# Two sets of q and k halves a layer, a loop over pairs of steps, and a new order of tasks in a two-layer attention kernel

## The chip, the cores and the metric

The kernel runs on one core of a Trainium2 chip. The metric is the device time of one execution in microseconds (us). The engines are PE (TensorE), ACT (ScalarE), DVE (VectorE), POOL (GpSimd) and SP (SyncE, which here only issues transfers). Each has its own in-order stream of instructions; they wait for one another through semaphores.

## The reference

Sixteen batches of x (256 rows of 512) go through four residual blocks; the context has 384 columns.

```python
x = x + _L0_xattn_ref(_layernorm(x, axis=-1), ctx_768, ctx_768, ...)   # q and k l2-normalised over 512, 16 heads of 32,
                                                                       # then out @ Wo + bo + Qp and a layer norm
x = x + _L0_ffn_ref(_layernorm(x, axis=-1), L0_ffn_weight)             # Hadamard, 4-bit levels per row, ternary weight
x = x + _L1_xattn_ref(_layernorm(x, axis=-1), ctx_768, ...)            # scores clipped, softmax, values, Wo
x = x + _L1_ffn_ref(_layernorm(x, axis=-1), W1, b1, W2, b2)            # ternary 512 -> 2048, gelu, ternary 2048 -> 512
```

## The kernel before

The first three blocks are one pipeline over batches, the last one (the FFN with 2048 columns) a second phase behind it, which the change doesn't touch. The rows of a batch are two tiles of 128 (`NT = 2`). Nearly all products are made of float16 halves: a value is split in an upper half (ACT rounds it) and a lower half (DVE subtracts), and three products are summed.

The work of a batch in the pipeline is four lists of tasks, the streams: 0 is layer 0's front (`front_0`: load of x and context, statistics, turns, projections of q, k and v, norms, turned and split q and k), 1 is layer 0's heads and back (`heads_of(0) + back(0)`: scores, exponentials, values, output projection, norm, then the Hadamard, level and ternary product of the small FFN, and the store of x1), 2 is layer 1's front (with `maxima`, products of scores only for the row maxima, and `reduce` on DVE), 3 is layer 1's heads and back (`clip` on DVE, `head`, output, store of x2). They are called 0f, 0b, 1f and 1b. In a step i of the pipeline 0f works on batch i, 0b on i-1, 1f on i-2 and 1b on i-3. Steps 0 to 3 are written out, steps 4 to 15 are a hardware loop (`steps`, `eng.Fori`), steps 16 to 18 are written out again with fewer streams active.

How the four lists are merged is a string of digits, `ORDER`: each digit says from which list the next task is taken. All engines walk the same merged list, and each issues its part of every task. The eight banks of PSUM are given out along this list too (`banks_of`): a task that fills a bank waits on PE until the bank's last reader is done (`open_bank`, semaphore `bankN_read`).

Task `head l n` is itself a small pipeline: ACT makes the exponential of head n (128x512 in float32, in a ring of `NF` buffers `pf`) and then the upper half (`ph`) of head n-1; POOL makes the lower half of head n-1 (L776); PE makes the product with the values for head n-4 (L1483 to L1485), and for layer 1 first a pair of products that subtracts the row maximum (L1465); DVE divides after every fourth head (`attn_out`, L1216, L1219). Scores come in quads of four heads, which use 32 rows of PE each (L1450).

The halves of turned q and k lie in one buffer a layer (`qk_raw`), so a batch's `split_qk` waits until the heads of the batch before are through (`p_hi`). Two buffers `spare` and a buffer `signs_raw` are used for weights: at the start for staging (`stage_w`), in steps 16 to 18 for the weights of the large FFN (`wb`, `wb_signs`), whose mean magnitude DVE sums in step 16 (`mean_part`, L1015, one at each second head of layer 0) and whose signs it makes in step 18. The levels of the small FFN, and then x1, are made in `tq`, which is the same memory as layer 0's attention output (`out0`).

Transfers: SP walks the same list. `load l` brings x and context (l = 0) or the context's turned halves and x1 (l = 1) of the batch, `fetch l` the residual of the back (and for l = 0 a copy of q inside SBUF); x1 is stored by POOL's queue (`store_x1`), x2 by SP's (L696).

## Time and profile before

| | |
|---|---|
| runs of the kernel | median 2068.04 us, 2066.56 to 2070.59 (3 runs) |
| the profiled execution | 2063.8 us, of which the span of the profile is 2062.1 |
| PE busy | 1787.1 us, 87% |
| DVE busy | 1333.4 us, 65% |
| ACT busy | 997.2 us, 48% |
| POOL busy | 897.2 us, 44% |
| PE, mean granted clock | 0.928 |

The shares are means over stages. PE's products are pipelined and their ends are modelled, so a product shows some 0.38 us where the next one starts after 0.22: the distance of starts tells what it costs. "issue" in place of a releaser means that the engine waited for nothing that the profile shows. Line numbers are those of the kernel before; a register wait shows as a row of kind ISA or REGISTER_ALU in the order.

### The profile page before, as it was taken

How to read it: one execution, taken by the hardware profiler on the slowest of the kernel's cores; microseconds unless marked ns; L12 is line 12 of the kernel's file. 1: busy time of each engine (PE TensorE's matmuls, PEld its weight loads, DVE VectorE, ACT ScalarE, POOL GpSimd, SP SyncE). 2: the span in 40 equal slices, each digit the busy share in tenths (PEclk: the TensorE clock that was granted, in tenths of full speed). 3: DMA queues.
4: the chain of work that ended last, by engine and by line, in shares of the span. 5: the costliest groups of instructions: out<-in, count | busy, mean ns of one | idle time of the engine just before them, and what ended most of it. 6: DMA issues, size and time to landing. Idle time of an engine off the chain costs nothing.

```text
span 2062.1 us, 49947 instructions
## 1 busy us (share of the span) xinstructions
PE 1787.1 (87%) x18714; PEld 1078.6 (52%) x18714; DVE 1333.4 (65%) x2518; ACT 997.2 (48%) x1858; POOL 897.2 (44%) x909
## 2 busy tenths in 40 slices
PE   4569898899988989889898899958746999999998
PEld 2335566565665756556565565635533444444443
DVE  4545787777877868778687786867586434444442
ACT  3534747566474665746657476544434222222221
POOL 1434638366382653737447374443423212222221
PEclk9679899998998999999999998969978999999999
DMA  4210202202021020210202112060232011111100
GB/s 161 98 49 27 86 12 87 71 27 97 2 96 71 27 97 1 97 70 28 96 2 97 55 43 96 2 233 1 91 128 72 1 42 41 41 41 41 41 21 21
DMA packets 48609, 124.12 MB, mean 60 GB/s; under 512 B 5644, under 2 KB 9868, under 8 KB 47384
## 3 DMA queue, kind: packets, MB, share of 16 engines
q1 hardware_dynamic: 46104, 112.64, 15.5%
q0 software_dynamic: 2304, 8.39, 1.0%
q8 instruction: 177, 2.90, 0.6%
q14 instruction: 24, 0.20, 0.0%
HBM read 81.17 MB, written 31.46 MB: 55 GB/s over the span
## 4 chain that ended last, share of the span: by engine, by line
PE 54%; DVE 19%; issue 11%; POOL 6%; DMA 4%; DVEq 2%; ACT 2%; SPq 1%; POOLq 0%; ACTq 0%
PE psum L1512 8%; PE psum L1502 8%; PE psum L1322 5%; PE psum L1302 5%; PE psum L1450 4%; PE psum L1303 4%; PE psum L1306 4%; POOL arena L776 3%; PE psum L1405 3%; DVE arena L1120 2%; DVE arena L1036 2%; DVEq L1037 2%; DMA arena<-in_ctx 2%; DVE psum L1130 2%; PE psum L1483 2%
## 5 line engine op out<-in xcount | busy, mean ns | idle before, releaser
L776 POOL TENSOR_TENSOR arena<-arena 128x512 f16<-128x512 f32 x512 | 565.2, 1127 | 242.3 <-ACT arena L924 240.0
L916 ACT ACTIVATE arena<-psum 128x512 f32<-128x512 f32 x512 | 307.3, 607 | 276.2 <-PE psum L1465 143.9
L924 ACT ACTIVATE arena<-arena 128x512 f16<-128x512 f32 x512 | 325.7, 642 | 6.8 <-PE psum L1485 6.3
L1302 PE MATMUL psum<-arena 128*128 128x512 f16 x672 | 262.0, 390 | 6.8 <-DVE arena L1047 6.3
L964 ACT ACTIVATE arena<-psum,arena 128x512 f32<-128x512 f32 x128 | 88.1, 688 | 361.3 <-PE psum L1502 361.3
L1303 PE MATMUL psum<-arena 128*128 128x512 f16 x672 | 259.4, 386 | 0.0
L1306 PE MATMUL psum<-arena 128*128 128x512 f16 x672 | 259.1, 386 | 0.0
L1512 PE MATMUL psum<-arena 128*128 128x512 f16 x1024 | 242.0, 378 | 8.9 <-DVE arena L1247 7.5
L1502 PE MATMUL psum<-arena 128*128 128x512 f16 x1024 | 243.0, 380 | 1.4 <-DVE arena L1235 1.4
L1483 PE MATMUL psum<-arena 128*128 128x33 f16 x2048 | 203.4, 182 | 41.6 <-POOL arena L776 39.6
L1450 PE MATMUL psum<-arena 32*128 32x256 f16 x4608 | 182.0, 293 | 62.6 <-issue 26.7
L1242 DVE CAST arena<-arena 128x512 f16<-128x512 f32 x128 | 72.4, 566 | 251.8 <-ACT arena L964 251.6
L806 POOL TENSOR_TENSOR arena<-arena 128x512 f16<-128x512 f32 x64 | 73.0, 1141 | 359.8 <-DVE arena L1242 359.8
L1322 PE MATMUL psum<-arena 128*128 128x128 f32 x992 | 165.6, 307 | 65.6 <-DMA arena<-in_ctx 28.2
L1483 PEld LDWEIGHTS psum<-arena 128*128 128x128 f16 x2048 | 173.5, 99 | 78.7 <-POOL arena L776 51.7
L1130 DVE TENSOR_SCALAR psum<-psum 128x512 f32<-128x512 f32 x256 | 163.3, 692 | 70.3 <-PE psum L1450 68.3
L1485 PE MATMUL psum<-arena 128*128 128x33 f16 x2048 | 199.4, 180 | 0.0
L1484 PE MATMUL psum<-arena 128*128 128x32 f16 x2048 | 199.2, 179 | 0.0
L858 ACT ACTIVATE arena<-psum 128x512 f16<-128x512 f32 (+1 forms) x192 | 110.0, 586 | 145.0 <-PE psum L1322 144.3
L1450 PEld LDWEIGHTS psum<-arena 32*128 32x128 f16 x4608 | 114.6, 99 | 123.5 <-issue 106.6
L1484 PEld LDWEIGHTS psum<-arena 128*128 128x128 f16 x2048 | 169.2, 99 | 11.1
L1322 PEld LDWEIGHTS psum<-arena 128*128 128x128 f32 x992 | 125.7, 156 | 93.3 <-issue 36.2
(117 smaller groups left out, 3255.0 us busy)
## 6 DMA issues: line engine op xcount, KB each, us to landing
arena<-x_scratch SPq DMA_DIRECT2D x48, 512.0 KB, 5.0
arena<-in_x SPq DMA_DIRECT2D x32, 512.0 KB, 5.8
arena<-in_L_ffn_W SPq DMA_DIRECT2D x16, 1024.0 KB, 5.2
arena<-arena SPq DMA_DIRECT2D x16, 512.0 KB, 5.7
x_scratch<-arena POOLq DMA_DIRECT2D x16, 512.0 KB, 3.9
x_scratch<-arena SPq DMA_DIRECT2D x16, 512.0 KB, 3.4
out<-arena SPq DMA_DIRECT2D x16, 512.0 KB, 3.2
arena<-in_ctx SPq DMA_DIRECT2D x16, 384.0 KB, 7.4
```

What stands on the lines that cost most here:

```text
L776: gp.tensor_tensor(pl[l][:, h % NP, :], pf[l][:, h % NF, :], ph[l][:, h % NP, :], ALU.subtract).then_inc(p_lo[l].sem, 1)
L916: sc.activation(pf[l][:, h % NF, :], bank(u.bank), ACT.Exp, scale=SCALE / (QS * QS) if l == 0 else SCALE).then_inc(read[u.bank], 1)
L924: sc.activation(ph[l][:, h % NP, :], pf[l][:, h % NF, :], ACT.Copy).then_inc(p_hi[l].sem, 1)
L1302: te.matmul(out, x_hi, w[:, 0, c, :], start=(c == 0), stop=False)
L1303: te.matmul(out, x_hi, w[:, 1, c, :], start=False, stop=False)
L1306: mm = te.matmul(out, x_lo, w[:, 0, c, :], start=False, stop=(c == chunks - 1))
L1322: mm = te.transpose(bank(u.bank)[:, c * P:(c + 1) * P], src[:, c * P:(c + 1) * P], ident)
L1450: mm = te.matmul(bank(u.bank)[:, k * S:(k + 1) * S], (qk_hi_t, qk_lo_t)[own][l][rows_g, j, m, k * P:(k + 1) * P], (qk_hi_t, qk_lo_t)[other ...
L1483: te.matmul(out, p_hi_t, vs[l][:, k, h, 0:OW], start=(k == 0), stop=False)
L1484: te.matmul(out[:, 0:HD], p_hi_t, vs[l][:, k, h, HD + 2:VP], start=False, stop=False)
L1502: mm = te.matmul(bank(4 + f % 2), w1T[:, c, f * P:(f + 1) * P], xTb[slot][:, part, c, :], start=(c + part == 0), stop=(c + part == DC))
L1512: mm = te.matmul(bank(k), src[:, f % NG, k * P:(k + 1) * P], w2T[:, f, :], start=(f + n == 0), stop=(f + n == FC))
```

## The change

- q and k halves: two sets a layer, chosen by the batch's parity (`halves`). `split_qk` now waits only for the heads of the batch two before. To choose the set at build time the loop's body holds two steps and runs six times.
- x1's sums and levels have a buffer of their own (`levels0`) instead of `out0`.
- The ring of exponentials `pf` has five buffers instead of four.
- To make room, `spare` and `signs_raw` are gone. Staging for weights at the start is in layer 1's halves; the large FFN's weights go through layer 0's first set and the memory of layer 0's q and k (`qk0`), which is free only when q has been copied.
- PE's waits for banks are merged where two of them concern the same bank.
- `ORDER` is a new string.

```diff
-ORDER = ("1103131313313331111010330110010000010011100110313301333133111313101331123333133311333331031230001233"
...
+ORDER = ("0211110211011300022120100100101010010111201030131000330310313031211330331332103113321212331133330132"
...
-    with eng.Fori(4, B) as i:
+    with eng.Fori(0, (B - 4) // 2) as r:
         if chain:
-            chain.offset = (i - 4) * per
-        since = {n: (i - 4) * n for n in sorted({n for x in both for n in x})}
-        emit(ALL, i, plan(ALL, base, [[since[n] for n in x] for x in both])[0])
+            chain.offset = r * (2 * per)
+        since = {n: r * (2 * n) for n in sorted({n for x in both for n in x})}
+        for odd in range(2):
+            uses = plan(ALL, plus(base, both, odd), [[since[n] for n in x] for x in both])[0]
+            emit(ALL, 2 * r + (4 + odd), odd, uses)
...
-        qk_raw = [take(2 * 2 * DC * S // 2) for _ in range(2)]
-        qk_hi_t, qk_lo_t = ([a.bitcast(F16).rearrange("p (s j m n) -> p s j m n", s=2, j=2, m=DC)[:, s] for a in qk_raw]
-                            for s in range(2))
+        qk_raw = [[take(2 * 2 * DC * S // 2) for _ in range(2)] for _ in range(2)]
+        qk_t = [[[a.bitcast(F16).rearrange("p (s j m n) -> p s j m n", s=2, j=2, m=DC)[:, s] for s in range(2)] for a in x]
+                for x in qk_raw]
         vs = [take(NT * H * VP // 2).bitcast(F16).rearrange("p (t h d) -> p t h d", t=NT, h=H) for _ in range(2)]
-        spare = [take(DC * D) for _ in range(2)]
-        signs_raw = take(DC * D)
-        NF, NP = 4, 4
+        levels0 = tiles(take(NT * D))
+        NF, NP = 5, 4
...
-        xp, tq = res0, out0
+        xp, tq = res0, levels0
...
+        def halves(l, odd, part):
+
+            return qk_t[l][(odd - ALL.index(part)) % 2]
+
...
-        stage_w = [a.rearrange("p (c n) -> p c n", c=DC) for a in spare]
+        stage_w = [a.rearrange("p (c n) -> p c n", c=DC) for a in qk_raw[1]]
...
-        wb = spare
+        wb = [qk_raw[0][0], qk0]
         wb_gt = ph_raw[0][:, 0:DC * D // 2].bitcast(F16)
-        wb_signs = [signs_raw[:, n * DC * D // 2:(n + 1) * DC * D // 2].bitcast(F16) for n in range(2)]
+        wb_signs = [qk_raw[0][1][:, n * DC * D // 2:(n + 1) * DC * D // 2].bitcast(F16) for n in range(2)]
...
                 if isinstance(i, int) and i == B:
-                    for n in range(2):
-                        load_wb(n)
+                    sp.wait_ge(p_hi[0].sem, p_hi[0].at(B - 2))
+                    load_wb(0)
...
                         fetch(l, b)
+                        if isinstance(i, int) and i == B and l == 0:
+                            sp.wait_ge(q_copied.sem, q_copied.at(B - 1))
+                            sp.wait_ge(qk_hi[0].sem, qk_hi[0].at(B - 1))
+                            load_wb(1)
...
                     elif kind == "split_qk":
-                        if not (isinstance(b, int) and b == 0):
-                            if l == 0 and at == [0, 0]:
-                                act.wait_ge(p_hi[0].sem, p_hi[0].at(b - 1))
-                            elif l == 1 and at[0] == 1:
-                                act.wait_ge(p_hi[1].sem, p_hi[1].at(b - 1, 2 * HG * (at[1] + 1)))
+                        if at == [l, 0] and not (isinstance(b, int) and b < 2):
+                            act.wait_ge(p_hi[l].sem, p_hi[l].at(b - 2))
...
                         act.wait_ge(absmax.sem, absmax.at(b, k + 1))
+                        if k == 0 and not (isinstance(b, int) and b == 0):
+                            act.wait_ge(x1_stored.sem, x1_stored.at(b - 1))
...
-                if g == 0 and l == 0 and not (isinstance(b, int) and b == 0):
-                    dve.wait_ge(x1_stored.sem, x1_stored.at(b - 1))
...
-            def open_bank(u):
-                if not (isinstance(u.free_at, int) and u.free_at == 0):
-                    pe.wait_ge(read[u.bank], u.free_at)
+            def open_banks(uses, after=()):
+
+
+                values = {u.bank: u.read_at for u in after}
+                values.update({u.bank: u.free_at for u in uses})
+                for n, value in values.items():
+                    if not (isinstance(value, int) and value == 0):
+                        pe.wait_ge(read[n], value)
+
+            def open_bank(u, *after):
+                open_banks([u], after)
...
                     elif kind == "values_ready":
-                        all_read(pe, [use["qkv", l, k, 2] for k in range(NT)])
-                        if l == 0:
-                            for k in range(NT):
-                                all_read(pe, [use["qt", 0, k, j] for j in range(2)])
+                        turned = [use["qt", 0, k, j] for k in range(NT) for j in range(2)] if l == 0 else []
+                        all_read(pe, turned + [use["qkv", l, k, 2] for k in range(NT)])
+                        pe.nop()
```

The order is seen in the engines' streams at three places. First the seam of two steps in the loop. PE, the first rows of a step; before, where L1450 is the quads of scores (layer 0, then layer 1) and L1465 the shift pair:

```order
L293 ISA
L1296 ISA [waits bank0_read]
L1296 ISA [waits bank1_read]
L1296 ISA [waits bank2_read]
L1450 MATMUL psum<-arena 128x256 [waits bank3_read]
L1450 MATMUL psum<-arena 128x256 x23
L1296 REGISTER_ALU
L1296 ISA [waits bank4_read]
L1296 REGISTER_ALU [waits bank5_read]
L1296 REGISTER_ALU [waits bank6_read]
L1450 MATMUL psum<-arena 128x256 [waits bank7_read]
L1450 MATMUL psum<-arena 128x256 x23
```

and of the change, where L1451 is the same quad and L1329 to L1333 a turned projection of layer 1's keys:

```order
L294 ISA
L1310 ISA [waits bank0_read]
L1310 ISA [waits bank1_read]
L1310 ISA [waits bank2_read]
L1451 MATMUL psum<-arena 128x256 [waits bank3_read]
L1451 MATMUL psum<-arena 128x256 x23
L1373 ISA
L1310 REGISTER_ALU [waits ctx_fetched]
L1329 MATMUL psum<-arena 128x256 [waits bank4_read]
L1331 MATMUL psum<-arena 128x256
```

Layer 1's scores have left the step's start, and two key projections of layer 1 (the second a little further on) stand there.

On DVE the same seam: the last rows of a step. Before (L1120 is `reduce`, L1146 the sum of layer 1's output):

```order
L1120 TENSOR_REDUCE arena<-psum 128x2 [waits bank7_filled]
L1119 REGISTER_ALU
L1120 TENSOR_REDUCE arena<-psum 128x2 [waits bank3_filled]
L1119 REGISTER_ALU
L1120 TENSOR_REDUCE arena<-psum 128x2 [waits bank1_filled]
L1120 TENSOR_REDUCE arena<-psum 128x2 [waits bank6_filled]
L1144 REGISTER_ALU [waits res_loaded_1]
L1146 SCALAR_TENSOR_TENSOR arena<-psum,arena 128x512 [waits bank5_filled]
L1144 REGISTER_ALU
L1146 SCALAR_TENSOR_TENSOR arena<-psum,arena 128x512 [waits bank4_filled]
```

and of the change (L1131 is `reduce`, L1105 the lower half of the values, L1194 the small FFN's output):

```order
L1105 SCALAR_TENSOR_TENSOR arena<-psum,arena 128x16x32 [waits v_hi_0]
L1193 REGISTER_ALU
L1194 SCALAR_TENSOR_TENSOR arena<-psum,arena 128x512 [waits bank2_filled]
L1130 REGISTER_ALU
L1131 TENSOR_REDUCE arena<-psum 128x2 [waits bank1_filled]
L1194 SCALAR_TENSOR_TENSOR arena<-psum,arena 128x512 [waits bank7_filled]
L1131 TENSOR_REDUCE arena<-psum 128x2 [waits bank4_filled]
L1131 TENSOR_REDUCE arena<-psum 128x2 [waits bank6_filled]
L1130 REGISTER_ALU
L1131 TENSOR_REDUCE arena<-psum 128x2 [waits bank5_filled]
```

The small FFN's output and so the store of x1 now come at the end of the step, and layer 1's output sums some 20 tasks ahead of it.

Second, SP in the loop. Before, the start of a step is `fetch 0`, then `load 0`, then `fetch 1`; `load 1` comes behind the store of the context:

```order
L639 ISA [waits x1_ready]
L639 DMA arena<-in_x 128x2x512
L640 ISA
L641 DMA arena<-arena 128x1024 [waits unit]
L652 ISA [waits qk_hi_0]
L652 DMA arena<-in_x 128x2x512
L653 ISA
L653 DMA arena<-in_ctx 128x2x384
L644 ISA
L645 ISA [waits x2_stored]
L645 DMA arena<-x_scratch 128x1024
```

and of the change, where `load 0` and `load 1` are first:

```order
L658 ISA [waits qk_hi_0]
L658 DMA arena<-in_x 128x2x512
L659 ISA
L659 DMA arena<-in_ctx 128x2x384
L662 ISA
L663 ISA [waits v_hi_1]
L664 ISA [waits ctx_stored]
L664 DMA arena<-ctx_scratch 128x768
L666 ISA [waits x1_stored]
L666 DMA arena<-x_scratch 128x1024
```

The two loads have moved ahead of the fetches, and with them the wait for the x1 store.

Third, SP at the start of step 16. Before:

```order
L613 DMA arena<-in_L_ffn_W 128x4x512 x2
L639 DMA arena<-in_x 128x2x512 [waits x1_ready]
L641 DMA arena<-arena 128x1024 [waits unit]
L645 DMA arena<-x_scratch 128x1024 [waits x2_stored]
L613 DMA arena<-in_L_ffn_W 128x4x512 [waits wb_used] x2
```

and of the change:

```order
L619 DMA arena<-in_L_ffn_W 128x4x512 [waits p_hi_0]
L664 DMA arena<-ctx_scratch 128x768 [waits ctx_stored,v_hi_1]
L666 DMA arena<-x_scratch 128x1024 [waits x1_stored]
L645 DMA arena<-in_x 128x2x512 [waits x1_ready]
L647 DMA arena<-arena 128x1024 [waits unit]
L619 DMA arena<-in_L_ffn_W 128x4x512 [waits qk_hi_0,q_copied]
L619 DMA arena<-in_L_ffn_W 128x4x512 [waits wb_used] x2
```

The second load of FFN weights has moved behind `load 1` and `fetch 0`.

## Rows read from the trace of the kernel before

**Rows 1.** Windows: the twelve loop steps, then four stretches of one step.

```profile
core 0: us, PE busy (x) PEld busy (x) DVE busy (x) ACT busy (x) POOL busy (x), PEclk, DMA share, GB/s
309.00:1351.00 1042.00, 955.57 (x12308) 627.85 (x12304) 795.01 (x1586) 643.18 (x1249) 568.81 (x600) 0.95 0.17 58
796.60:829.50 32.90, 32.82 (x278) 19.55 (x278) 27.14 (x55) 12.70 (x24) 4.21 (x5) 1.00 0.04 14
830.00:846.00 16.00, 10.73 (x186) 7.10 (x186) 7.57 (x16) 13.71 (x28) 11.50 (x12) 0.68 0.55 193
846.00:862.00 16.00, 15.84 (x313) 11.65 (x314) 10.54 (x24) 15.23 (x32) 15.34 (x15) 1.00 0.24 84
```

**Rows 2.** Timeline of SP: stores of x2, at the ends of steps 3, 15, 16, 17.

```profile
309.30 0.34 SPq L696 DMA_DIRECT2D x_scratch<-arena  x1
...
1350.79 0.36 SPq L696 DMA_DIRECT2D x_scratch<-arena  x1
1451.38 0.35 SPq L696 DMA_DIRECT2D x_scratch<-arena  x1
1512.30 0.35 SPq L696 DMA_DIRECT2D x_scratch<-arena  x1
```

**Rows 3.** The chain that ended last: start us, us on the chain, what.

```profile
798.53 0.87 PE psum L1322 x8
799.41 1.73 PE psum L1405 x8
801.57 0.11 PE psum L1312
815.05 0.77 PE psum L1450 x24
855.11 0.23 PE psum L1465 x2
```

**Rows 4.** Timeline of PE: first and last of 24 products with the values.

```profile
787.61 0.18 PE L1483 MATMUL psum<-arena 128*128 128x33 f16 x1
...
788.19 0.18 PE L1485 MATMUL psum<-arena 128*128 128x33 f16 x1
```

**Rows 5.** Timeline of POOL among the heads.

```profile
842.79 7.81 POOL L776 TENSOR_TENSOR arena<-arena 128x512 f16<-128x512 f32 x7
```

**Rows 6.** Timeline of PE: the loop's entry, and one jump back.

```profile
309.55 0.71 PE L1450 MATMUL psum<-arena 32*128 32x256 f16 x17 [0.34 <-DVE arena L1146]
...
830.84 1.48 PE L1450 MATMUL psum<-arena 32*128 32x256 f16 x45 [1.39 <-issue]
834.19 0.40 PE L1450 MATMUL psum<-arena 32*128 32x256 f16 x3 [1.87 <-issue]
```

**Rows 7.** List of waits: us in total, times, longest.

```profile
PE psum L1322 <- DMA arena<-in_ctx: 28.2, 13, 11.5
PE psum L1450 <- issue: 26.7, 22, 1.9
```

**Rows 8.** Timeline of DVE: a run of reduces.

```profile
825.81 3.24 DVE L1120 TENSOR_REDUCE arena<-psum 128x2 f32<-128x512 f32 x5
```

**Rows 9.** The page's DMA issues: KB each, median us to landing.

```profile
arena<-x_scratch SPq DMA_DIRECT2D x48, 512.0 KB, 5.0
...
arena<-in_L_ffn_W SPq DMA_DIRECT2D x16, 1024.0 KB, 5.2
arena<-arena SPq DMA_DIRECT2D x16, 512.0 KB, 5.7
x_scratch<-arena POOLq DMA_DIRECT2D x16, 512.0 KB, 3.9
...
arena<-in_ctx SPq DMA_DIRECT2D x16, 384.0 KB, 7.4
```

**Rows 10.** Timeline of DVE in step 16: first and last of eight.

```profile
1357.60 2.29 DVE L1015 TENSOR_REDUCE arena<-arena 128x1 f32<-128x2048 f32 x1 [6.86 <-DMA arena<-in_L_ffn_W]
...
1385.61 2.29 DVE L1015 TENSOR_REDUCE arena<-arena 128x1 f32<-128x2048 f32 x1 [1.63 <-DMA arena<-in_L_ffn_W]
```

**Rows 11.** DVE's normalise by line: duration ns min/median/max.

```profile
L1041 DVE TENSOR_SCALAR arena<-arena x128: 519/549/1464, 19.6 to 1976.7; 128x512 f32<-128x512 f32 x128
```

More of the change, by code:

```diff
@@ L283, in alone @@
         uses, counts = plan(active, base, None)
-        emit(active, i, uses)
+        emit(active, i, i % 2, uses)
         return plus(base, counts)
@@ L903, in step @@
                             j, m = at
-                            sc.activation(qk_hi_t[1][:, j, 2 * m:2 * m + 2, :], bank(u.bank).rearrange("p (m n) -> p m n", m=2),
+                            sc.activation(upper[:, j, 2 * m:2 * m + 2, :], bank(u.bank).rearrange("p (m n) -> p m n", m=2),
                                           ACT.Copy, scale=1.0 / WS).then_inc(qk_hi[1].sem, 1)
@@ L1103, in step @@
                         u = use["qt", l, at[0], at[1]]
+                        upper, lower = halves(l, odd, part)
                         if l == 0:
@@ L1107, in step @@
                             cols_k = slice(k * P, (k + 1) * P)
-                            v.tensor_tensor(qk_lo_t[0][:, j, :, cols_k], bank(u.bank).rearrange("p (m n) -> p m n", m=DC),
-                                            qk_hi_t[0][:, j, :, cols_k], ALU.subtract).then_inc(read[u.bank], 1)
+                            v.tensor_tensor(lower[:, j, :, cols_k], bank(u.bank).rearrange("p (m n) -> p m n", m=DC),
+                                            upper[:, j, :, cols_k], ALU.subtract).then_inc(read[u.bank], 1)
                         else:
@@ L1317, in product_turned, with turn @@
                 return mm
-            def turn(u, src, chunks):
-                open_bank(u)
+            def turn(u, src, chunks, after=()):
+                open_bank(u, *after)
                 for c in range(chunks):
@@ L1323, in turn, with step @@
                 mm.then_inc(filled[u.bank], 1)
-            def step(active, i, use):
+            def step(active, i, odd, use):
                 for part, (kind, l, *at) in task_order(active):
@@ L1372, in step @@
                     elif kind == "maxima":
-                        if k % 2 == 0:
-                            all_read(pe, [use["qt", 1, j, k // 2] for j in range(2)])
-                        products_of_quad(1, k, 0, [use["mx", 1, h] for h in quad(k)])
+                        products_of_quad(halves(1, odd, part), k, 0, [use["mx", 1, h] for h in quad(k)],
+                                         [use["qt", 1, j, k // 2] for j in range(2)] if k % 2 == 0 else [])
                     elif kind == "scores":
@@ L1378, in step @@
                             pe.wait_ge(setup_act, DC + 1)
-                        products_of_quad(l, k, 1, [use["s", l, h] for h in quad(k)])
+                        products_of_quad(halves(l, odd, part), k, 1, [use["s", l, h] for h in quad(k)])
                     elif kind == "head":
@@ L1382, in step @@
                     elif kind == "turn_out":
-                        if k == 0:
-                            all_read(pe, [use["o", l, g] for g in range(H // HG)])
-                        turn(use["ot", l, k], attn[l][:, k, :], DC)
+                        turn(use["ot", l, k], attn[l][:, k, :], DC, [use["o", l, g] for g in range(H // HG)] if k == 0 else [])
                     elif kind == "out_project":
@@ L1398, in step @@
                     elif kind == "hadamard":
-                        u = use["xf", 0, k]
-                        pe.wait_ge(read[u.bank], u.read_at)
                         u = use["had", 0, k]
-                        open_bank(u)
+                        open_bank(u, use["xf", 0, k])
                         for c in range(DC):
@@ L1415, in step @@
                     elif kind == "ffn0":
-                        u = use["nt", 0, k]
-                        pe.wait_ge(read[u.bank], u.read_at)
                         u = use["f0", 0, k]
-                        open_bank(u)
+                        open_bank(u, use["nt", 0, k])
                         for c in range(DC):
@@ L1439, in step, with products_of_quad @@
                     all_read(pe, [use["y", 1, k] for k in range(NT)])
-            def products_of_quad(l, m, j, uses):
-                for u in uses:
-                    open_bank(u)
+            def products_of_quad(parts, m, j, uses, after=()):
+                open_banks(uses, after)
                 for k in range(NT):
```

44 lines of the change are left out of this document (19 added, 25 removed).

## The prediction

> **What bounds the kernel now.** I read the stretches by engine first. Over the twelve steps of the main loop PE is busy for 955.57 of 1042 us and DVE for 795.01, while ACT and POOL stay near 60% [rows 1]. The stores of x2, one a step, give the step: from 309.30 to 1350.79 there are twelve, 86.8 us each; the two steps behind take 100.6 and 60.9 [rows 2].
>
> How much of 86.8 is PE's own work? From the distances of starts in the chain [rows 3]: a 512-column product takes 0.217 us (1.73 for eight), a 256-column one 0.11, a fp32 turn of 128 columns 0.109, a quad of scores 0.77, a shift pair 0.23; of the small products of values and exponentials 24 take 0.60 us, 0.025 each [rows 4]. A full step has 158 products of 512 columns (134 in projections, 16 Hadamard, 8 FFN): 34.2 us; 92 of 256: 10.0; 12 quads: 9.3; 384 small ones: 9.6; 62 fp32 turns: 6.8; 16 shift pairs: 3.7; 8 small turns: 0.5. Sum 74.1 us. Changes of form cost something too: from the Hadamard product at 796.6 to the step's end at 829.5 PE is busy for 32.82 of 32.90 us at full clock [rows 1], where the counts give 32.3. With that and a little more for the short groups among the heads I take a floor of 77.3 us. So about 9.5 us a step are lost, nearly all in the other part of the step.
>
> Where: from 830 to 846 PE is busy for only 10.73 of 16 us and at a granted clock of 0.68, while ACT has 13.71 and POOL 11.50; from 846 to 862 ACT has 15.23 in 32 instructions and POOL 15.34 [rows 1]. That is the run of heads, where a head costs ACT two instructions, 1.0 us, and POOL 1.12 us (7.81 for 7) [rows 5]. Up to layer 0's head 9 the order of before gives PE four quads, four shift pairs, six heads' values and two turns: 3.1 + 1.0 + 2.1 + 0.7, 7 us of work. ACT gets 14 exponentials, 12 copies and two context copies, 14 us, and POOL 12 heads and a variance, also 14. PE must wait for some 7 us, whatever stands behind. In PE's timeline two stalls of 1.39 and 1.87 with no releaser lie where the loop jumps back [rows 6]. By the list of waits the pair stands at 11 edges, 26.7 us in 22, or 2.43 an edge [rows 7]; at the loop's entry, reached without a jump back, 0.34 stands there [rows 6], with some 0.8 behind it that is DVE's.
>
> **The change, part by part.** *The order.* Up to the same head 9 PE's work is now three quads 2.3, two turned key projections (20 products each) 4.4, four turns 1.5, six heads' values 2.1, and the first half of a key projection 1.3: 11.6 us. ACT has ten exponentials and nine copies, 9.5, and six evacuations at a little over 0.5: 13. POOL has 9 heads and one variance, 11. The mismatch falls from 7 to about 1.4. Further on (layer 1's head 4) my running sums are PE 26, ACT 27, POOL 26: no engine is idle by design, but three in-order engines hand work to each other at every head, and each hand-over can cost. Nothing of this kind is in a row of before, where in that part only ACT and POOL are full; the bounds are 0 and the 5.27 us that PE lost from 830 to 846. I take 3.0, the clock included: above the middle, since all three are full for longer.
>
> *The seam.* Behind the first Hadamard product DVE has 16 reduces, thirteen sums and splits, two maxima with their small chains: at 0.648 us for a reduce (3.24 for five) [rows 8] and little more for the others 24 us. PE has 19.3 behind the second, 1.7 us later: DVE sets the end. Walked through with these prices, and the second Hadamard product's end as 0, PE's last product ends at 19.3; the bank that the next scores need last (bank 1, DVE's reduce behind the first FFN sum) comes free at 20.05, and after 0.8 of scores bank 4 comes free 0.55 later: 1.3 us a step.
>
> *Pairs of steps.* Five jumps back instead of eleven. A jump's 2.43 now lies over the 1.3 of the seam, so it adds 1.1, five times in twelve steps: 0.5. That the loop's body is twice as long I take at nothing: the steps ahead of the loop run straight on, and no such pair of stalls lies there. The Trainium skill (Runtime: NRT & Kernel Launch, Instruction fetch mechanics) says that instructions are fetched ahead only in sequence and that a taken branch out of the fetched window is what stalls; by that a body that never fitted costs nothing more when it doubles. No run here shows that yet.
>
> *Two sets of halves, the x1 buffer, the ring of five.* They take away no wait that I find among the rows of before; they are what lets the projections of layer 1 and the sums stand where they now do. Extra work: none. The merged bank waits take PE's register rows from 115 to about 95 a step, on a sequencer that is behind only at the edge: 0.
>
> *SP's queue.* x and context are now the first loads of a step and wait only for layer 0's last upper half, 30 tasks before the end. PE's waits for context, 28.2 us in 13 [rows 7], should go; they lie within the 9.5. Against that, layer 1's load stands ahead of the fetches and waits for the x1 store. The last sum is ready 2 us after the first scores; the store lands 3.9 us after its issue, the load after 5.0, or 7.4 as the context does now in such a crowd [rows 9]: x1 arrives at 13 to 15 us. DVE comes to its statistics behind head 12, at PE's 16th us. It fits, by one to three.
>
> So a step takes 77.3 + 3.0 + 1.3 + 0.5 = 82.1 us, and twelve give 985, 56 less than 1041.5. The three steps ahead of the loop have the same layer-0 half and the same late loads; I take 4.6 for the full one and 3 for each of the others, 11 less.
>
> *The end.* Step 16 gets worse. The means of the FFN weights block DVE: the first starts at 1357.60 after 6.86 us of waiting, the eighth ends at 1387.9, 37 us after the step's start [rows 10, 2]. Now only one staging buffer is free at once. The other is layer 0's q and k, free when the copy of q has landed: x1 stored (at 7), loads, the copy (issued at 8.5, 5.7 to land), then 1 MB (5.2 or more) [rows 9]: about 21 us for the second mean. The six behind it keep the 4.0 us of now, so the row ends near 47, +10. Step 17 has layer 1's two streams only; there the projections now lie beside the heads instead of behind them, at the price of 9 us of waiting for x1 at the statistics: between -12 and +9, I take -4. Step 18 holds one stream, whose own order is the same, and the FFN is untouched: 0.
>
> Sum: -56 - 11 + 10 - 4 = -61. The profiled execution takes 2063.8 (span 2062.1): 2003. The median of the runs is 4.2 higher, so **2007 us**.
>
> **A rule that speaks against it.** DVE's normalise (128x512, fp32) takes 549 ns in the median and up to 1464 [rows 11]; the long ones lie where POOL works on heads. In the new order layer 1's two are moved from behind the heads into them, 0.9 us longer each, 1.8 a step. There DVE has by my count 22 us of work against PE's 26, so the row makes it 0. The Trainium skill (GPSIMD Engine Reference, Specifications) says that GpSimd shares its SBUF interfaces with VectorE and contends with its two-port modes and with two SBUF inputs. By it POOL would be held too, and POOL has no slack there: 1.8 us on the path.
>
> **The rivals.**
> - *Denser than I think* (0.14). The hand-overs cost 1 and not 3, the seam nothing: 78.8 a step, -96 in the loop, -17 ahead: about 1961. For it: PE ran for 32.8 us without a gap beside a DVE at 82% [rows 1].
> - *The clock falls in the dense part* (0.10). Now it is at half for part of the slow stretch, where PE waits anyway. If a fall follows a seam or a jump and meets 6 us of dense work, it costs 3 us a step: 85.1, so -20 in the loop, 2043 with the rest.
> - *DVE and POOL hold each other* (0.05): 1.8 us a step on the path, +22: 2029.
> - *Nothing gained* (0.05). The light stretch of heads is only moved to where DVE sets the pace: 2068.
> - *Slower* (0.10). DVE stands at layer 1's statistics until x1 is there; clips, sums and biases of both layers queue behind it, and PE follows within two heads. From x1 at 16 us on, each microsecond costs one a step; past 20.7 it has eaten the gain. At 23 a step takes 88.5: +20 in the loop, nothing won ahead of it, +6 at the end, 2094. For it: four transfers of 512 KB lie at that place. Against it: their median landings [rows 9].
>
> **How the numbers follow.** The forecast above has 0.56, its own range is 1987 to 2029. A measurement here tells 0.2%, 4 us, from no change. Faster: 0.56 + 0.14 + 0.10 + 0.05 = 0.85; same 0.05; slower 0.10. The range leaves out the slower case, no gain, and the densest end: 1960 to 2052.
>
> **What would show it.** Stores of x2 some 82 us apart, alternating by a microsecond with the jump; PE's waits for context gone; in the 16 us behind a step's start PE above 14 busy and the clock near 1; the pair of stalls without releaser at the jumps only; step 16 above 105 us. I am wrong if DVE waits for x_scratch at its statistics for over 2 us, if PE's gaps lie at the values of heads, or if the clock is below 0.9 in the dense part.

## The result

The changed kernel takes 2004.21 us (median of 4 runs, 2002.49 to 2005.34) where the kernel before takes 2069.32 (4 runs): ratio 0.9686, 95% interval 0.9669 to 0.9703. Its profiled execution has a span of 2003.5 us against 2062.1, so 58.6 us less.

The page of the kernel after:

```profile
PE 1763.9 (88%) x18714; PEld 1061.7 (53%) x18714; DVE 1379.2 (69%) x2518; ACT 985.2 (49%) x1858; POOL 897.2 (45%) x909
...
PEclk9689999999999999999999999969869999999999
```

All engines run as many instructions as before. PE is busy 23 us less although it does the same products; its clock was granted at 0.947 in the mean against 0.928, and the clock digits of the loop are all 9.

Which part gave what? I cut both traces at the first scores of each step (PE's L1450, after L1451), and ahead of step 17, which has no scores of layer 0, at the end of step 16's last quad.

| stretch | before, us | after, us | difference | predicted |
|---|---|---|---|---|
| step 0 | 61.8 | 67.7 | +5.9 | 0 |
| steps 1, 2, 3 | 79.2, 82.2, 85.2 | 75.1, 67.8, 80.6 | -4.2, -14.4, -4.6 | -11 together |
| loop, steps 4 to 15 | 1041.4 | 1001.0 | -40.5 | -56 |
| steps 16 and 17 | 162.7 | 166.0 | +3.3 | +10 and -4 |
| step 18 and FFN | 549.6 | 545.5 | -4.2 | 0 |

The sum is right and its terms are not: they miss by +5.9, -12.2, +15.5, -2.7 and -4.2 us, which cancel to +2.3. That the total of 2007 us came within 3 us of the measured 2004.2 is luck of that kind. Both the loop and the steps ahead of it have to be explained.

From here on single steps of the loop are measured from one store of x2 to the next. In the changed kernel this store stands 7 us ahead of the next step's first scores (1285.08 and 1292.10), before it stood 1 us behind them (1350.79 and 1349.81), so the two cuts divide the ends of the pipeline differently.

Windows of after: the twelve loop steps, from store to store (the row that answers to the first of [rows 1]).

```profile
core 0: us, PE busy (x) PEld busy (x) DVE busy (x) ACT busy (x) POOL busy (x), PEclk, DMA share, GB/s
283.90:1285.08 1001.18, 942.53 (x12290) 615.53 (x12288) 833.21 (x1585) 632.58 (x1248) 568.64 (x600) 0.97 0.18 61
```

That is 83.4 us a step. The stores of x2 of three steps in a row, the second of which crosses a jump back:

```profile
366.95 0.35 SPq L706 DMA_DIRECT2D x_scratch<-arena  x1
...
447.63 0.35 SPq L706 DMA_DIRECT2D x_scratch<-arena  x1
...
533.25 0.34 SPq L706 DMA_DIRECT2D x_scratch<-arena  x1
...
615.61 0.35 SPq L706 DMA_DIRECT2D x_scratch<-arena  x1
```

80.68, 85.62, 82.36. Leaving out the first interval, 83.05, which crosses the loop's entry, the six within a pair are 80.68 to 82.38 (mean 81.8) and the five across a jump 85.09 to 86.04 (mean 85.5): a jump costs 3.7 us, not the 1.1 that I had put on it. Windows of the same three intervals, PE alone:

```profile
core 0: us, PE busy (x), PEclk, DMA share, GB/s
366.95:447.63 80.68, 76.70 (x1025) 1.00 0.18 62
447.63:533.25 85.62, 79.75 (x1025) 0.96 0.18 60
533.25:615.61 82.36, 78.39 (x1025) 0.98 0.18 61
```

Two costs show. Across this jump PE is busy 3.05 us longer than in the interval before it for the same products, because the granted clock falls, and idle some 1.9 us longer. The third interval has a small fall of the clock without a jump: 1.7 us. Four of the six intervals within a pair are of this kind, so in the mean a jump's 3.7 us are 1.7 of busy time (79.5 against 77.8) and 2.0 of idle time (6.0 against 4.0). PE's timeline at a jump of after (as in [rows 6]):

```profile
954.99 1.04 PE L1424 MATMUL psum<-arena 128*128 128x512 f16 x4
959.42 1.43 PE L1451 MATMUL psum<-arena 32*128 32x256 f16 x24 [3.39 <-issue]
...
962.47 0.42 PE L1332 MATMUL psum<-arena 128*128 128x256 f16 x1
962.68 0.40 PE L1333 MATMUL psum<-arena 128*128 128x256 f16 x1
962.89 0.30 PE L1329 MATMUL psum<-arena 128*128 128x256 f16 x1
963.02 0.27 PE L1331 MATMUL psum<-arena 128*128 128x256 f16 x1
963.13 0.27 PE L1332 MATMUL psum<-arena 128*128 128x256 f16 x1
```

PE stands for 3.39 us with no releaser. Behind it products of 256 columns start every 0.21 us until about 962.9, and every 0.11 after that: half the clock (1.2 GHz of 2.4) for some 3.5 us. DVE has the same stand, [2.88 <-issue] at 961.86. So the jump stops both engines.

The list of waits of after, PE (us in total, times, longest):

```profile
PE psum L1451 <- issue: 16.1, 6, 3.4
```

The 26.7 us in 22 stalls of before [rows 7] became 16.1 in 6, of which five are at the jumps (2.91 to 3.39 each) and one of 0.59 is in step 16. PE's waits for context, 28.2 us in 13 [rows 7], are down to one of 11 us ahead of the loop.

Ahead of the loop, windows of step 2, of before and then of after:

```profile
140.99:223.18 82.19, 63.94 (x670) 0.87 0.15 49
```

```profile
142.71:210.54 67.83, 58.55 (x670) 1.00 0.17 58
```

Of the 14.4 us that step 2 gained, 5.4 are PE's own products at full clock instead of 0.87, and 9.0 are waits that went (3.90 for the context, 3.25 for ACT's exponentials among them).

### The profile page after: what moved, and what is told of

It reads as the page before. It is cut to its first block and busy times, and to the rows that moved or that the text cites. A ratio compares the mean times of both kernels' runs of the same rounds, so it can differ in the third digit from the quotient of the medians.

```text
span 2003.5 us, 49343 instructions
## 1 busy us (share of the span) xinstructions
PE 1763.9 (88%) x18714; PEld 1061.7 (53%) x18714; DVE 1379.2 (69%) x2518; ACT 985.2 (49%) x1858; POOL 897.2 (45%) x909
## 5 line engine op out<-in xcount | busy, mean ns | idle before, releaser
L786 POOL TENSOR_TENSOR arena<-arena 128x512 f16<-128x512 f32 x512 | 586.1, 1165 | 248.7 <-ACT arena L932 248.0
L816 POOL TENSOR_TENSOR arena<-arena 128x512 f16<-128x512 f32 x64 | 73.0, 1140 | 357.0 <-DVE arena L1251 357.0
L1451 PE MATMUL psum<-arena 32*128 32x256 f16 x4608 | 170.3, 280 | 58.2 <-DVE arena L1124 17.1
L1484 PE MATMUL psum<-arena 128*128 128x33 f16 x2048 | 200.5, 179 | 16.6 <-POOL arena L786 16.5
L1486 PE MATMUL psum<-arena 128*128 128x33 f16 x2048 | 197.8, 178 | 0.0
L1484 PEld LDWEIGHTS psum<-arena 128*128 128x128 f16 x2048 | 171.5, 97 | 49.5 <-POOL arena L786 21.1
L798 POOL TENSOR_TENSOR arena<-arena 128x512 f32<-128x512 f32 x32 | 40.5, 1267 | 340.9 <-DVE arena L1194 339.3
L1339 PE MATMUL psum<-arena 128*128 128x128 f32 x992 | 148.3, 288 | 44.9 <-DVE arena L1057 12.5
L1131 DVE TENSOR_REDUCE arena<-psum 128x2 f32<-128x512 f32 x256 | 163.8, 684 | 20.2 <-PE psum L1451 20.2
L1485 PEld LDWEIGHTS psum<-arena 128*128 128x128 f16 x2048 | 166.0, 98 | 10.7 <-issue 0.3
L1513 PEld LDWEIGHTS psum<-arena 128*128 128x128 f16 x1024 | 98.5, 97 | 126.6 <-DVE arena L1256 11.4
L1141 DVE TENSOR_SCALAR psum<-psum 128x512 f32<-128x512 f32 x256 | 160.2, 688 | 7.8 <-PE psum L1451 7.7
```

The source lines that it names most:

```text
L786: gp.tensor_tensor(pl[l][:, h % NP, :], pf[l][:, h % NF, :], ph[l][:, h % NP, :], ALU.subtract).then_inc(p_lo[l].sem, 1)
L1451: mm = te.matmul(bank(u.bank)[:, k * S:(k + 1) * S], parts[own][rows_g, j, m, k * P:(k + 1) * P], parts[other][rows_g, 1 - j, m, :], start ...
L1484: te.matmul(out, p_hi_t, vs[l][:, k, h, 0:OW], start=(k == 0), stop=False)
L1485: te.matmul(out[:, 0:HD], p_hi_t, vs[l][:, k, h, HD + 2:VP], start=False, stop=False)
L1486: mm = te.matmul(out, p_lo_t, vs[l][:, k, h, 0:OW], start=False, stop=(k == NT - 1))
L1513: mm = te.matmul(bank(k), src[:, f % NG, k * P:(k + 1) * P], w2T[:, f, :], start=(f + n == 0), stop=(f + n == FC))
```

## The experiments

### The jump back

The first experiment gives the loop over pairs to the kernel before, and nothing else.

```diff
-    with eng.Fori(4, B) as i:
+    with eng.Fori(0, (B - 4) // 2) as r:
...
+        for odd in range(2):
+            emit(ALL, 2 * r + (4 + odd), plan(ALL, plus(base, both, odd), ...)[0])
```

> The kernel before, with only its main loop changed to two steps an iteration: 5 jumps back instead of 11, nothing else. Theory A: a jump costs about 3.7 us wherever it stands (in the changed kernel the stores of x2 are 85.5 us apart over a jump and 81.8 without one), so 6 fewer give -22 us: about 2046. Theory B, the one of the prediction: a jump's stall mostly lies over waiting that is there anyway, net 1.3 us each: -8 us, about 2060. The stores of x2 should alternate by 3.7 or by 1.3 us.

Measured: 2061.29 us, ratio 0.9979 (0.9967 to 0.9991), span 2056.3. PE's stalls without releaser at L1451 fell from 26.7 us in 22 to 12.4 in 10, but from store to store the loop is only 3.2 us shorter, 0.5 for each of the six jumps saved. The intervals alternate by more than that: those across a jump are 87.4 us in the mean, those within a pair 85.8 (leaving out the one that crosses the loop's entry). So in the old order a jump costs 0.5 us by the loop's length and 1.6 by the alternation; by either it is not 3.7, and Theory B, 1.3, is the nearer one. The next kernel is the changed one without any jump.

```diff
-    with eng.Fori(0, (B - 4) // 2) as r:
...
+    for i in range(3, B):
+        base = alone(ALL, i)
```

> The changed kernel with its twelve loop steps written out: no jump back, no waits on registers. Theory A: only the jumps cost, 5 times 3.7 us: -18.5 us against the changed kernel, about 1986, and every step takes 81.8 us. Theory B: register arithmetic or the fetch of the longer body cost too: then every step gets shorter than 81.8, or longer if straight code is fetched too slowly (over 2004).

Measured: 1981.47 us, ratio 0.959 (0.9555 to 0.9625), span 1982.5, 21 less than with the jumps. The twelve intervals of x2 stores are 80.66 to 82.65, mean 81.53. The step of my forecast without its jump term, 77.3 + 3.0 + 1.3 = 81.6, is what is left. The loop alone is 22.9 us shorter from store to store, of which 2.4 are in its first interval and 20.5 in the eleven that held the jumps: 4.1 a jump. The doubled or twelvefold body costs nothing that shows: of PE's stalls without releaser at the scores 0.5 us are left. The Trainium skill's rule (Runtime: NRT & Kernel Launch, Instruction fetch mechanics), that a taken branch out of the fetched window is what stalls the fetch, agrees with it. That the stand is a fetch and nothing else done at a jump is not shown. And what does writing out do to the kernel before?

> The kernel before with its twelve loop steps written out, so with no jump at all, and nothing else. My theory (in the old order a jump costs 1.3 to 1.5 us of the step, because TensorE would stand for the light stretch of heads anyway; only in the new order nothing covers it and it costs 3.7 to 4): 11 jumps by 1.4, 15 us less: 2052 +-4 us. Rival A (a jump costs 3.7 us in either order): 41 us less, 2027 us. Rival B (the loop over pairs already took all that there is): 2061 us.

Measured: 2060.91 us, ratio 0.997 (0.9959 to 0.998), span 2059.0. So my own theory was too high here as well. The loop fell from 1041.5 to 1030.9 us, 1.0 a jump; 3.1 of this came back in step 16 (103.7 us from store to store against 100.6), so 0.3 to 0.6 us a jump reached the end. The windows of the start of a step show why. Before, in [rows 1], PE had 10.73 of 16 us, at clock 0.68. Written out, the same step starts at 824.11:

```profile
825.00:841.00 16.00, 10.91 (x179) 7.94 (x180) 8.58 (x17) 14.91 (x30) 13.32 (x14) 0.70 0.55 189
```

Without any jump PE has no more than 10.91 us there and the clock is 0.70, because PE waits for others instead. Its timeline:

```profile
832.34 0.21 PE L1472 MATMUL psum<-arena 128*128 128x33 f16 x1 [1.97 <-POOL arena L765]
835.14 0.90 PE L1311 MATMUL psum<-arena 128*128 128x128 f32 x3 [1.42 <-DMA arena<-in_ctx]
```

So in the old order the jump lies over waits for POOL and for the context, and its fall of the clock over one that the light stretch brings on anyway. The new order takes this cover away, and both costs come out: a jump costs 0.5 to 1.0 us of the loop under cover (1.6 by the alternation in the pairs) and 3.7 to 4.1 in the open.

### The order and the buffers

The changed kernel with the `ORDER` of before (all else as changed: halves, x1 buffer, ring, pairs, merged waits):

> The changed kernel with the old order of tasks: both sets of halves, the buffer for x1, the ring of five, merged waits and the loop over pairs, but the tasks merged as before. Theory A: the buffers take no wait away by themselves; what is left is the saved jumps and the worse staging in step 16: the time of e1_pairs plus up to 12 us, 2046 to 2058. Theory B: the buffers are worth something without the order: clearly below e1_pairs.

Measured: 2063.79 us, ratio 0.9988 (0.9975 to 1.0001), span 2062.1. The steps are 86.4 us and PE's clock is 0.924. Everything but the order is worth nothing that this measurement can tell. Both theories missed: the time lies above the range of A too. The trace has two parts that cancel: from store to store the loop is 5.2 us shorter than before (in e1_pairs, with the jumps alone, 3.2), and step 16 takes 105.85 us instead of 100.59, which is the price of the worse staging.

So the gain is the order's. But the string moves two things at once: the tasks of the engines, and with them SP's loads, which now come first in a step. No kernel here separates them. DVE's list of waits before has this line, one wait of 2.5 to 6.3 us in each step of the loop:

```profile
DVE arena L1036 <- DMA arena<-in_x: 64.0, 15, 10.8
```

In the changed kernel DVE waits for no load of x in the loop, and PE's 28.2 us of waits for the context [rows 7] are gone from it as well. How much of the gain is the earlier load and how much the closer mix of heads and projections stays open.

Then the buffers one at a time in the new order. The ring of four:

```diff
-        NF, NP = 5, 4
+        NF, NP = 4, 4
```

> The changed kernel with its ring of exponentials cut back from five to four buffers and nothing else. My theory (the ring is no limit; the new order alone shortens the loop): 2004 +-3 us, intervals between x2 stores of 81 to 82 us within a pair and 85 to 86 over a jump, as with five. Rival (the fifth buffer lets ScalarE run further ahead in the dense stretch, and the new order needs it): ScalarE waits for a free buffer, TensorE's attention products wait for the exponentials, and the steps are 0.5 us or more longer, 2011 us or above.

Measured: 1999.84 us, ratio 0.9672 (0.9653 to 0.9691). The fifth buffer gives nothing; the interval overlaps that of the changed kernel. x1's sums in `out0`:

```diff
-        xp, tq = res0, levels0
+        xp, tq = res0, out0
...
+                if g == 0 and l == 0 and not (isinstance(b, int) and b == 0):
+                    dve.wait_ge(x1_stored.sem, x1_stored.at(b - 1))
```

> The changed kernel with the sums of x1 back in the buffer that the normalised heads of layer 0 use (the wait for x1's store stands ahead of the first normalisation of heads again), and nothing else. My theory (the store has long landed when those heads begin): 2004 +-3 us, VectorE waits for no DMA in the loop. Rival (in the new order layer 0's first heads come closer behind the store of x1): VectorE waits up to 2 us a step there and hands this to TensorE, 2020 us or above.

Measured: 2001.77 us, ratio 0.9682 (0.9665 to 0.97). The store has landed when the heads begin; this buffer gives nothing either. And PE's waits for banks one by one:

```diff
-                values = {u.bank: u.read_at for u in after}
-                values.update({u.bank: u.free_at for u in uses})
-                for n, value in values.items():
+                for n, value in [(u.bank, u.read_at) for u in after] + [(u.bank, u.free_at) for u in uses]:
```

> The changed kernel with every wait for a PSUM bank issued by itself again, where the changed kernel waits once for each bank; nothing else. My theory (TensorE's sequencer has room everywhere but at the jumps): 2004 +-3 us, with perhaps 0.1 us more at a jump. Rival (the merged waits are part of the gain: the sequencer falls behind at the quads and the turned tiles): gaps with no releaser at those places and 2010 us or above.

Measured: 2006.33 us, ratio 0.9705 (0.9687 to 0.9722), span 2006.4 against 2003.5. At the scores 16.8 us in 6 stand without releaser instead of 16.1. The median is 0.1% higher and the interval overlaps that of the changed kernel, so it can't be told from nothing. The new order with a single set of halves was not tried: its splits would have to wait for the heads of the batch before, which is another kernel. Whether the second set is needed for the new order stays open.

### Step 16

I expected step 16 to lose 10 us to the sums of the FFN weights. It takes 98.5 us by the cuts of the table, where before it took 101.5; from store to store it is 100.71 against 100.59. Timeline of after's DVE, and then of its PE:

```profile
1294.98 2.29 DVE L1025 TENSOR_REDUCE arena<-arena 128x1 f32<-128x2048 f32 x1
1311.86 2.29 DVE L1025 TENSOR_REDUCE arena<-arena 128x1 f32<-128x2048 f32 x1 [14.60 <-DMA arena<-in_L_ffn_W]
...
1319.53 2.29 DVE L1025 TENSOR_REDUCE arena<-arena 128x1 f32<-128x2048 f32 x1 [2.00 <-DMA arena<-in_L_ffn_W]
```

```profile
1317.64 1.47 PE L1451 MATMUL psum<-arena 32*128 32x256 f16 x24 [17.07 <-DVE arena L1124]
...
1330.73 1.47 PE L1451 MATMUL psum<-arena 32*128 32x256 f16 x24 [5.91 <-DVE arena L1228]
```

The second sum starts 19.8 us behind the first scores at 1292.10 (I had said about 21), and holds all that DVE has behind it: PE waits 17.07 and 5.91 us. The last of the eight starts at 1335.1 and ends 45 us behind those scores, where I had said 47. In the next kernel two sums stay among the heads of layer 0 (heads 1 and 16) and six go among those of layer 1:

```diff
-        mean_at = (B, {("head", 0, 1 + 2 * n): n for n in range(2 * WC)})
-        mean_done_at = (B, {("head", 0, 2 * (2 * WC)): 0})
+        mean_at = (B, {task: n for n, task in enumerate([("head", 0, 1), ("head", 0, 16)] + [("head", 1, 3 + 3 * n) for n in range(6)])})
+        mean_done_at = (B, {("head", 1, 19): 0})
```

> The changed kernel, where in step 16 the sums of the magnitudes of the large FFN's weights stand later in DVE's stream: the first at layer 0's head 1 as now, the second at layer 0's head 16, the other six at every third head of layer 1. Theory A: PE's stall of 17.07 us at the start of step 16, in which DVE waits for the second staging buffer, and the 5.9 us behind it set the step's end: -15 to -22 us, about 1985. Theory B: step 16 is bound by its chain of dependent work and DVE's 18.3 us of sums in any place: less than 5 us.

Measured: 1983.64 us, ratio 0.9597 (0.9572 to 0.9622), span 1986.5. Step 16 takes 84.88 us from store to store where the changed kernel needs 100.71, and DVE's list of waits has none for these weights left. So the block by the weights is real: without it step 16 is 15.8 us shorter, and the span 17.0. PE's two waits were 23.0 us together, so some 7 of them were caught up within the step. My term of +10 took the old step 16 as it was and added to it. Two runs take that apart. The new staging in the old order makes step 16 5.3 us longer (105.85 against 100.59), half of my term; and with that staging the new order makes it 5.1 us shorter (100.71), which I had put at nothing.

### Step 0

Nothing in the diff touches the tasks of step 0, yet it lost 5.9 us. Only stream 0 is active there, but the banks are dealt out along the merged order of all four. By that order the first turned tile of the context and of x and the first k projection all get bank 2, and the second tile of x and the first q projection bank 4; before, they had 5, 0, 5 and 4, 3. PE's timeline before and after:

```profile
20.21 1.97 PE L1322 MATMUL psum<-arena 128*128 128x128 f32 x8 [7.16 <-DVE arena L1041]
22.89 0.59 PE L1302 MATMUL psum<-arena 128*128 128x512 f16 x1 [0.71 <-DVE arena L1047]
```

```profile
22.82 1.94 PE L1339 MATMUL psum<-arena 128*128 128x128 f32 x8 [10.07 <-DVE arena L1057]
29.97 0.58 PE L1319 MATMUL psum<-arena 128*128 128x512 f16 x1 [5.22 <-DVE arena L1057]
```

The turns of x start 2.6 us later and the first product of the projections 7.1 us later, because they wait for splits that they did not wait for before. The next kernel deals the banks of step 0 out from its own tasks:

```diff
+FIRST_BANK_OF = banks_of([task for task in TASKS if PART[task] == "0f"], POOLS)
...
-    bank_of = BANK_OF if len(active) > 1 or "1b" not in active else LAST_BANK_OF
+    bank_of = BANK_OF if len(active) > 1 else LAST_BANK_OF if "1b" in active else FIRST_BANK_OF
```

> The changed kernel with PSUM banks for step 0 dealt out from that step's own tasks, where the changed kernel takes over the banks that the order of all four streams gives them (there the first turned tile of the context, the first turned tile of x and the first projection all share one bank). Nothing is computed otherwise. My theory (the 5.9 us that step 0 lost come from this sharing: each of these tasks waits until VectorE and ScalarE have read the one before): the first scores of step 1 come at about 60 to 62 us instead of 67.7, and the time is 1996 to 1999 us. Rival (step 0 is held by the splits of the inputs and weights on VectorE, which no bank changes): first scores at 67 to 68 us, 2004 us.

Measured: 1998.98 us, ratio 0.9663 (0.9646 to 0.968), span 1997.2 against 2003.5. The times alone overlap those of the changed kernel; the trace decides. The turns of x are back at 19.83 and the first scores stand at 62.38 instead of 67.66:

```profile
19.83 1.97 PE L1340 MATMUL psum<-arena 128*128 128x128 f32 x8 [7.27 <-DVE arena L1052]
22.51 0.59 PE L1320 MATMUL psum<-arena 128*128 128x512 f16 x1 [0.71 <-DVE arena L1058]
```

The other traces agree. In all six kernels with the shared banks the first scores stand at 65.5 to 67.7 us, in the six without them (the old order, or banks dealt anew) at 59.7 to 62.5.

### All three together

> The changed kernel with three things at once: the twelve steps of the loop written out, the sums over x2 for the mean spread over step 16 later, and the banks of step 0 dealt out from its own tasks. My theory (jumps, sums before layer 1's statistics and shared banks are three separate losses of 20.7, 20.6 and about 6 us): 1957 +-5 us. Rival (the losses overlap, because a step that follows a jump or a stall catches up what it lost): 1970 us or above.

Measured: 1959.94 us, ratio 0.948 (0.9451 to 0.951), span 1962.1. The spans of the three alone were 21.0, 17.0 and 6.3 below the changed kernel's, 44.3 together; the measured 41.4 are nearly that sum. The three losses lie apart. This is the fastest version, 5.2% below the kernel before.

## Why the prediction was right, and where it was not

**What bounds the kernel.** Right. PE's floor of 77.3 us is the 76.55 to 76.70 that it is busy in a step at full clock, and the 9.5 us that I called lost were idle and half-clock time in the run of heads. Windows of after, 16 us behind a step's start, the first within a pair, the second behind a jump (columns as in [rows 1]):

```profile
875.00:891.00 16.00, 14.79 (x237) 10.85 (x235) 11.80 (x22) 14.45 (x30) 14.59 (x15) 1.00 0.55 191
959.00:975.00 16.00, 15.48 (x220) 11.28 (x221) 8.98 (x16) 13.65 (x28) 11.29 (x12) 0.89 0.55 193
```

Above 14 busy, as predicted, where [rows 1] had 10.73; across the jump the window begins behind most of the stand, and its clock is 0.89, just under the 0.9 that I had named as a sign of being wrong. Within a pair it is 1.00.

**Hand-overs 3.0 and seam 1.3.** Right as a sum. In the step of 80.68 us PE is idle for 3.98, in gaps of which these are the largest at the seam and behind it:

```profile
374.09 0.84 PE L1451 MATMUL psum<-arena 32*128 32x256 f16 x24 [0.23 <-DVE arena L1131]
...
375.40 0.27 PE L1329 MATMUL psum<-arena 128*128 128x256 f16 x1 [0.47 <-DVE arena L1131]
...
407.09 0.39 PE L1319 MATMUL psum<-arena 128*128 128x512 f16 x1 [1.46 <-DVE arena L1057]
...
423.88 0.39 PE L1466 MATMUL psum<-arena 128*128 128x256 f16 x2 [0.99 <-DVE psum L1141]
```

The first two are the seam, 0.7 us where I had 1.3; the large ones wait for turned x (L1057) and at a shift pair (L1141), in the middle of the step. The mean of 81.8 has the clock's small falls in it: 1.1 us, which my 3.0 was to include, so that hand-overs, seam and clock are 5.1 where I had 4.3, on a floor that is 76.7 where I had 77.3. These two misses nearly cancel as well.

**The jumps, 0.5 us a step.** This is the step that failed. I read 2.43 us an edge from the list of waits, took 1.3 of it as covered by the seam, and put the clock at nothing without a reason. Behind a jump of after PE's timeline has:

```profile
457.46 1.24 PE L1451 MATMUL psum<-arena 32*128 32x256 f16 x24 [2.91 <-issue]
...
468.28 0.84 PE L1451 MATMUL psum<-arena 32*128 32x256 f16 x24 [0.16 <-DVE arena L1057]
```

The stand is 2.91 us here and 3.1 in the mean of the five. It does cover something: of the waits that a step within a pair has at its start, 0.23, 0.47, 0.28 and 0.23 us, only 0.16 is left, so 1.05 are covered where I had 1.3. The idle time that a jump adds is thus 2.0 us instead of 1.1. The rest, 1.7, is the clock that falls behind the stand. Together 3.7 us, five times: 18.5 us of loop where I had 5.5. That is 13 of the some 16 us by which the loop missed; 8.5 of the 13 are the clock and 4.5 the stand. Another 1.3 lie in the loop's first interval, 83.05, in which PE waits 1.46 us for the context's turned halves, and the rest in steps of 81.8 instead of 81.6. The rival "the clock falls in the dense part" had the mechanism (a fall behind a jump that meets dense work) with 3 us in every step. It comes behind every jump, and in four of the six steps within a pair behind a wait of 1.46 us, where it costs 1.7.

**Three steps ahead, -11.** Under-sized: -23.2 for steps 1 to 3. I scaled by the loop's gain, and step 2, where layer 1 has only its front, lost most to the late context and had a clock of 0.87. Step 0 gave back 5.9, through banks, which I had costed at nothing because its tasks did not move.

**The end.** The block in step 16 was right in place and time (45 us against 47), its price wrong as told above, and the sign that I gave, step 16 above 105 us, did not come. Step 17 did not gain 4 us but lost 6.3 by the cuts of the table, 3.2 from store to store: PE is busy for 48.6 us from store to store, 44.5 before, and its first product of layer 1 waits 4.63 for the context's halves. I had that stream's wait in view, at the wrong transfer. No experiment was made on it; the other kernels with the new order take 61.1 to 63.4 us for this step from store to store, before it was 60.9. Step 18 and the FFN gained 4.2, where I had 0; no experiment touched them.

**At nothing.** The ring, the x1 buffer and the merged waits gave nothing, each by a kernel of its own; the second sets of halves gave nothing in the old order; the doubled body cost nothing, by the kernel written out.

**The rule on shared interfaces.** My premise for it was wrong. The two normalises of layer 1 (DVE's L1051, two in one row) were to become 0.9 us longer each; before and after they take:

```profile
797.11 1.00 DVE L1041 TENSOR_SCALAR arena<-arena 128x512 f32<-128x512 f32 x2
```

```profile
899.92 1.11 DVE L1051 TENSOR_SCALAR arena<-arena 128x512 f32<-128x512 f32 x2
```

The median over all 128 normalises did rise from 549 ns [rows 11] to 946, in after by line (duration ns min/median/max):

```profile
L1051 DVE TENSOR_SCALAR arena<-arena x128: 518/946/1460, 19.5 to 1918.1; 128x512 f32<-128x512 f32 x128
```

But this median misleads. The durations lie in two clusters, below 0.7 us and above 0.9 with nothing between them: before 68 and 60 of the 128, after 63 and 65. The few that changed sides moved the median across the gap. The mean went from 901 to 896 ns. The groups of DVE before and after, by line (the second number behind the bar is the mean):

```profile
L1041 DVE TENSOR_SCALAR arena<-arena 128x512 f32<-128x512 f32 x128 | 111.5, 901 | 30.3 <-POOL arena L751 29.1 <-POOL arena L756 1.0
```

```profile
L1051 DVE TENSOR_SCALAR arena<-arena 128x512 f32<-128x512 f32 x128 | 110.9, 896 | 27.4 <-POOL arena L761 26.4 <-POOL arena L766 1.0
```

What separates them is POOL: in after the 65 normalises that lie wholly beside POOL instructions take 934 to 1460 ns, the 34 with none beside them 534 to 548. This agrees with the Trainium skill (GPSIMD Engine Reference, Specifications), which has the two engines share their interfaces to SBUF. POOL's group of the page:

```profile
L786 POOL TENSOR_TENSOR arena<-arena 128x512 f16<-128x512 f32 x512 | 586.1, 1165 | 248.7 <-ACT arena L932 248.0
```

Its mean was 1127 ns before, 38 ns less a product. Whether that is DVE's doing was not taken apart, nor whether part of PE's wait of 1.46 us for turned x comes from it.

**The slower case** did not come: in the pipeline DVE has no wait for x1 at its statistics (the list's 11.3 us in 6 for x_scratch all lie behind 1600 us, in the large FFN), only the 14.8 us in five stands at the jumps.

## What to carry to other kernels

A cost that is covered is not small: price it as if its cover were gone, above all when the change is there to take the cover away. With the new order a jump back went from 0.5 to 1.0 us of the loop to 3.7. Where anything is dealt out along one list (banks, buffers), a new order changes also the stages that run only part of that list; compare each stage of the trace, not only the total, since here five wrong terms added up to a right sum. And look at a mean beside a median: where durations lie in two clusters, the median can rise by 70% while the mean stays.

## What the runs showed of the hardware

In the changed kernel a jump back of the loop stops PE for 2.9 to 3.4 us and DVE for 2.8 to 3.1 with nothing to wait for; in the kernel before PE stands in two pieces, 2.4 us together in the mean. In the changed kernel TensorE's granted clock is at half behind the jump, for some 3.5 us in three of the five and for some 6 in two (0.50 from 793.29 to 799.00 and from 1127.48 to 1133.60). It can fall without a jump as well, behind a short wait, and not each time. Timelines of the kernel written out, first a step of 80.67 us and then one of 82.34:

```profile
651.23 0.39 PE L1306 MATMUL psum<-arena 128*128 128x512 f16 x1 [1.40 <-DVE arena L1044]
651.46 0.38 PE L1307 MATMUL psum<-arena 128*128 128x512 f16 x1
651.67 0.38 PE L1310 MATMUL psum<-arena 128*128 128x512 f16 x1
...
812.56 0.51 PE L1306 MATMUL psum<-arena 128*128 128x512 f16 x1 [1.40 <-DVE arena L1044]
812.86 0.63 PE L1307 MATMUL psum<-arena 128*128 128x512 f16 x1
813.29 0.63 PE L1310 MATMUL psum<-arena 128*128 128x512 f16 x1
```

Both wait 1.40 us for the same split. Behind one the products start every 0.22 us, behind the other every 0.43 for 3.3 us, which costs 1.67 us of the step. That is the whole difference between the two levels, 80.7 and 82.3, at which nine of the twelve steps lie. The same wait leads to either; which of the two comes is fixed by something that I did not find: two kernels written out, one starting 4 us earlier than the other, have the same sequence of levels.
